# Binary block: the downward product in two halves, and another order of the maxima, clips and output additions

## What is computed

```python
def _quantize_activations_groupwise(x):          # NUM_GROUPS = 5, groups of the batch
    for g in range(NUM_GROUPS):
        ag = x[g * gs:(g + 1) * gs]
        gamma = jnp.max(jnp.abs(ag))
        xq = xq.at[g * gs:(g + 1) * gs].set(jnp.clip(ag * QB / (gamma + EPS), -QB + EPS, QB - EPS))
...
h = _bitlinear(x, W1, b1)          # x @ sign-like W1 + b1, then the quantisation above
h = jax.nn.gelu(h, approximate=False)
out = _bitlinear(h, W2, b2)        # the same again, back to 96 channels
...
t = t + _L2_ffn_ref(_ln_t(t), L2_ffn_W1, L2_ffn_b1, L2_ffn_W2, L2_ffn_b2)
```

## Time and profile before

| | us |
|---|---|
| median of 3 runs | 1110.09 (1109.1 to 1111.11) |
| the profiled execution | 1110.88 |
| its span, first to last instruction | 1109.1 |
| the binary block in it, first upward product to last residual | 689.93 to 771.56 |

### The profile page before, as it was taken

One profiled execution on the slowest core, in us unless ns is written; L12 is line 12 of the kernel. 1 busy time (PEld: TensorE's weight loads), 2 busy tenths in 40 slices (PEclk: granted clock), 3 DMA queues, 4 the chain that ended last, 5 costly groups with the idle time before them and its releaser, 6 DMA issues. The chain is left out here.

```text
span 1109.1 us, 29005 instructions
## 1 busy us (share of the span) xinstructions
PE 1006.5 (91%) x11022; PEld 681.8 (61%) x11022; DVE 676.6 (61%) x1880; ACT 610.5 (55%) x1662; POOL 593.2 (53%) x788
## 2 busy tenths in 40 slices
PE   5999989799979799999999997787988988999998
PEld 2677755467745476767676765455665565566665
DVE  2899944499956355656566663576776686433332
ACT  1666633367733366666666663545665564456553
POOL 4667538477665355454545446344465545373632
PEclk9999999899989999999999998889999999999999
DMA  6500000000000000000000000000000000000000
GB/s 126 97 6 2 2 1 3 1 1 3 1 2 2 1 1 1 2 1 2 1 1 1 2 2 1 2 1 2 1 1 2 2 1 2 2 16 9 16 9 16
DMA packets 28248, 9.65 MB, mean 9 GB/s; under 512 B 26513, under 2 KB 28112, under 8 KB 28112
## 3 DMA queue, kind: packets, MB, share of 16 engines
q1 hardware_dynamic: 25088, 6.89, 3.0%
q10 hardware_dynamic: 3024, 0.92, 0.4%
HBM read 6.23 MB, written 1.57 MB: 7 GB/s over the span
## 5 line engine op out<-in xcount | busy, mean ns | idle before, releaser
L1140 POOL TENSOR_TENSOR fa_e<-fa_e,fa_rc 128x1024 f32<-128x1024 f32 x64 | 120.5, 1893 | 142.3 <-DVE fa_rc L1363 142.3
L1653 POOL TENSOR_TENSOR ca_e<-ca_e,ca_rc 128x256 f32<-128x256 f32 x96 | 76.7, 826 | 84.0 <-DVE ca_rc L1978 84.0
L1297 ACT ACTIVATE fa_e<-bank,fa_nm 128x256 f32<-128x256 f32 x256 | 118.6, 497 | 0.0
L1884 ACT ACTIVATE ca_e<-bank,ca_nm 128x128 f32<-128x128 f32 x192 | 78.0, 430 | 51.0 <-DVE ca_nm L1964 51.0
L2183 ACT ACTIVATE ex_G<-bank,e_b 128x512 f32<-128x512 f32 x96 | 64.4, 687 | 50.2 <-PE bank L137 47.5
L137 PE MATMUL bank<-hT,e_w 96*64 96x512 f32 x384 | 88.6, 596 | 0.0
L2255 DVE SCALAR_TENSOR_TENSOR X<-bank,ex_L,X 128x96 f32<-128x96 f32 x128 | 31.7, 310 | 88.9 <-PE bank L137 82.4
L1357 DVE TENSOR_REDUCE fa_nm<-bank 128x4 f32<-128x1024 f32 x64 | 75.5, 1219 | 14.6 <-PE bank L1166 14.6
L137 PEld LDWEIGHTS bank<-e_w,ex_G 128*64 128x64 f32 x1536 | 67.2, 137 | 17.2 <-issue 10.5
L167 POOL TENSOR_TENSOR ln_r<-ln_v,minus_half 128x2 f32<-128x2 f32 (+2 forms) x85 | 75.7, 890 | 0.0
L186 DVE TENSOR_TENSOR X<-X,bank 128x192 f32<-128x192 f32 (+1 forms) x72 | 30.0, 418 | 71.8 <-PE bank L137 54.2
(11 more groups left out here) (247 smaller groups left out, 2395.1 us busy)
## 6 DMA issues: line engine op xcount, KB each, us to landing
out_tokens<-X SPq DMA_DIRECT2D x8, 192.0 KB, 2.1
X<-in_x SPq DMA_DIRECT2D x14, 96.0 KB, 3.2
e_w<-in_L_ffn_w SPq DMA_DIRECT2D x2, 576.0 KB
bias0r<-in_L_conv_rpb_table ACTq DMA_DIRECT2D x16, 24.0 KB
m0w<-in_L_conv_mlp_w SPq DMA_DIRECT2D x2, 144.0 KB
m1w<-in_L_conv_w SPq DMA_DIRECT2D x2, 144.0 KB
f_w<-in_L_ffn_W SPq DMA_DIRECT2D x2, 142.5 KB
mixer<-in_mixer SPq DMA_DIRECT2D x1, 256.0 KB
```

The costliest lines, as they stand in the source:

```text
L1140: pool.tensor_tensor(e, e, r.broadcast_to([P, 4, TOK]), ALU.mult).then_inc(s["nrm"], 1)
L1297: last = act.activation(E[v % 4][:, i, c, :], bank[b + i][:, c * TOK:(c + 1) * TOK], ACT.Exp, bias=NM[v % 4][:, i, c:c + 1], accum_out=SU[ ...
L1653: last = pool.tensor_tensor(e, e, RC[u % 2][:, images, c, :].broadcast_to([P, 2, (c + 1) * P]), ALU.mult)
L1884: last = act.activation(E[u % 2][:, j, keys(c)], bank[j][:, keys(c)], ACT.Exp, bias=NM[u % 2][:, j, c:c + 1], accum_out=SU[u % 2][:, j, c: ...
```

## The change

- The maximum of the hidden values is taken for each chunk, as soon as the two biases of the chunk are there, into three columns of `parts`; a last reduction makes `am` from them. A semaphore `part` is added.
- The downward product is split: `down(g, b)` does three tiles into bank 6 + b and increments `down` for each half, and the waits on `down` count two a group.
- TensorE's order in iteration g is now: units 4 and 5 of up of g; transposes of g + 1; first half of down of g - 1; spread of the hidden maximum of g; second half of down of g - 1; units 0 to 3 of up of g + 1; `keep_warm` into bank 0; spread of the output maximum of g - 1. The wait for all biases is gone, as is the hidden spread's wait for the output additions. In the first iteration `keep_warm` stands ahead of the spread, into bank 6.
- VectorE's order is now: maximum of g; clips of g; output additions and maximum of g - 1; the rest of the output of g - 1.

```diff
-        def down(g):
+        def down(g, b):
             pe.wait_ge(s["gelu"], KH * (g + 1))
             after(pe, s["z"], 2 * g)
             after(pe, s["ar2"], g)
-            for t in range(GT):
+            for t in range(3):
...
+        up(0, 0, 4)
         for g in range(GROUPS + 1):
             if g < GROUPS:
-                up(g)
+                up(g, 4, 2)
             if g + 1 < GROUPS:
                 tokens(g + 1)
             if g >= 1:
-                down(g - 1)
+                down(g - 1, 0)
             if g < GROUPS:
-                pe.wait_ge(s["h"], 6 * (g + 1))
-                keep_warm(pe, k, bank[2][:], 4)
+                if g == 0:
+                    keep_warm(pe, k, bank[6][:], 4)
                 pe.wait_ge(s["am"], g + 1)
-                after(pe, s["z"], 2 * g)
                 spread(0, 6).then_inc(s["bc1"], 1)
+            if g >= 1:
+                down(g - 1, 1)
+            if g + 1 < GROUPS:
+                up(g + 1, 0, 4)
+                keep_warm(pe, k, bank[0][:], 4)
             if g == GROUPS:
                 next(run)
             if g >= 1:
                 pe.wait_ge(s["am2"], g)
                 spread(1, 7).then_inc(s["bc2"], 1)
...
         def hidden_max(g):
-            dve.wait_ge(s["h"], 6 * (g + 1))
+            for j in range(KH):
+                dve.wait_ge(s["h"], 6 * g + 2 * j + 2)
+                dve.tensor_reduce(parts[:, j:j + 1], H[g % 2][:, j, :], AX.X, ALU.max, apply_absolute_value=True).then_inc(s["part"], 1)
+            dve.wait_ge(s["part"], KH * (g + 1))
             after(dve, s["bc1"], g)
-            dve.tensor_reduce(am[:, 0:1], H[g % 2][:], AX.XY, ALU.max, apply_absolute_value=True).then_inc(s["am"], 1)
+            dve.tensor_reduce(am[:, 0:1], parts[:], AX.X, ALU.max).then_inc(s["am"], 1)
...
         def output(g):
-            dve.wait_ge(s["down"], g + 1)
             after(dve, s["x"], g)
             for b in range(2):
+                dve.wait_ge(s["down"], 2 * g + b + 1)
...
             if g < GROUPS:
                 hidden_max(g)
+                hidden_clip(g)
             if g >= 1:
                 output(g - 1)
-            if g < GROUPS:
-                hidden_clip(g)
-            else:
+            if g == GROUPS:
                 next(run)
             if g >= 1:
                 quantised_output(g - 1)
```

More of the change, by code:

```diff
@@ L216 @@
 LN_SEMS = "var centred rstd y xb x bn ag mv "
-BF_SEMS = LN_SEMS + "tw twe T hT up h am bc1 ar1 c1 clip gelu down z am2 bc2 ar2 c2 zc top0 inv0 top1 inv1"
+BF_SEMS = LN_SEMS + "tw twe T hT up h part am bc1 ar1 c1 clip gelu down z am2 bc2 ar2 c2 zc top0 inv0 top1 inv1"
 CA_SEMS = LN_SEMS + "init T hT ab abe abd vt v sc nm exp rec nrm et ete av ote pj oc bt"
@@ L1430, in binary_ffn @@
     am, ar, cc = sb("am", [P, 2]), sb("ar", [P, 2]), sb("cc", [P, 2, 4])
+    parts = sb("parts", [P, KH])
     half = GT * P // 2
@@ L1455, in tensor, with up @@
     def tensor(pe):
-        def up(g):
+        def up(g, first, count):
             pe.wait_ge(s["hT"], g + 1)
[L1459 to L1463, removed]
-        def down(g):
+            for u in range(first, first + count):
+                j, i = divmod(u, 2)
+                after(pe, s["h"], 6 * g + u - 3)
+                halves(pe, bank[2 + u % 4][:, 0:half], w1T[:, j * P:(j + 1) * P], hT[:, i * half:(i + 1) * half], start=True, stop=True).then_inc(s["up"], 1)
+        def down(g, b):
             pe.wait_ge(s["gelu"], KH * (g + 1))
@@ L1468, in down @@
             after(pe, s["ar2"], g)
-            for t in range(GT):
+            for t in range(3):
                 for j in range(KH):
-                    last = halves(pe, bank[6 + t // 3][:, (t % 3) * C:(t % 3 + 1) * C], H[g % 2][:, j, t * P:(t + 1) * P], w2T[:, j, :],
+                    last = halves(pe, bank[6 + b][:, t * C:(t + 1) * C], H[g % 2][:, j, (3 * b + t) * P:(3 * b + t + 1) * P], w2T[:, j, :],
                                   start=(j == 0), stop=(j == KH - 1))
@@ L1527, in scalar @@
         for g in range(GROUPS):
-            after(act, s["down"], g - 1)
+            after(act, s["down"], 2 * (g - 1))
             for j in range(KH):
```

## The result

The changed kernel takes 1117.15 us (median of 9 runs, 1113.12 to 1118.33) where the kernel before, on the same chips, takes 1111.13: a ratio of 1.0059, 95% interval 1.0047 to 1.0072. It is slower by 6.0 us; 1111.2 and a range of 1107 to 1115 had been forecast. The profiled execution took 1118.01 us with a span of 1116.2.

The account below looks back on a forecast made before the run. No engine was full: a ring of waits bound the kernel, with VectorE losing 2.15 us behind the downward product. Terms -3.70, +4.11, -0.40, +1.10 gave +1.11 us on the median of 1110.09: 1111.2, range 1107.0 to 1115.0.

Parts of the forecast that it names:

- the sum: Whole block: -3.70 up to the last hidden-maximum spread, then +4.11, -0.40 and +1.10, giving +1.11 us.
- The first period: From first to second hidden-maximum spread: VectorE's maximum ready earlier, TensorE free at 9.05; 9.1 against 13.22 us, -4.12.
- the low stretch set aside: Between first and second hidden-maximum spreads: low clock on transposes and half product would make the gain up to 1.4 us less.
- the term for the clock: At the block's end: half clock on the attention's eight transposes behind two idle times, +1.1 us, bounds 0 and 1.65.
- First spread: Start of the block: with the maximum in three parts, the first hidden-maximum spread comes at 698.99 instead of 700.39, -1.40 us.
- Second to fourth period: Later hidden-spread periods: TensorE's queue and low clock hold the output spread; 13.12, 14.49, 14.49 us: -0.15, +1.17, +0.80.
- Extra 0.27 for the parts: VectorE's maximum in each later period: three more instructions cost 0.27 to 0.35 us of the 12.36 us row.
- The end: After the last hidden-maximum spread: attention transposes wait for the output maximum, +4.11; first-half additions overlap, -0.40; clock, +1.1 us.
- low clock twice: Rival, late periods: two low stretches in succession move the output spread from 7.03 to 8.7; +3.3, 1114.5 us; chance 0.25.
- Full clock: Rival, late periods and end: denser filling keeps TensorE fast; periods 13.12 and 13.86, 1108.1 us; chance 0.2.
- the end is covered: Rival, block's end: the following stage doesn't wait for the attention's start, so the 4.11 don't show; 1107.1 us; chance 0.1.

Follow-up runs that it names:

- the run without the four products: The changed kernel without the four filler products (`keep_warm` into bank 0) ahead of the output maximum's spread; 1114.66 us, 1.0035 to the kernel before.
- the run with filler: The changed kernel with twelve more filler products behind the downward product's first half from the third group on; 1114.80 us, 1.0037 to the kernel before.
- The run with the end undone: The changed kernel, with the attention's transposes and first three projections ahead of the output-maximum wait in the last iteration; 1113.47 us, 1.0023 to the kernel before.
- three edits: The changed kernel with attention work ahead of the last wait, no filler ahead of the output spread, filler in TensorE's idle times; 1108.65 us, 0.999 to the kernel before.

## Why the prediction was wrong

In the block the sum gave +1.11 us and +5.27 was measured. Two steps make up the difference. The first period was priced at full clock, with the low stretch set aside without a reason and GpSimd not looked at: 2.18 us. At the end the term for the clock, +1.10, measured 3.56. The other terms came within 0.4 us each, most of them shorter.

- **First spread**: right, 1.32 us against 1.40. Only the last part, 0.95 us, and the last step, 0.16, stood ahead of SP0; the first two parts were taken while TensorE still made the later units.
- **First period, 9.1 forecast, 11.28 measured**: the first step that failed. Its two terms, about 1.5 and 0.7 us, show in the timeline of the changed kernel and in the clock of the stretch:

```profile
704.42 1.51 PE L137 MATMUL bank<-bf_hT,bf_w1T 96*64 96x384 f32 x8 [1.91 <-ACT bf_H L1538]
705.86 1.34 PE L1479 MATMUL bank<-ident,Y 128*96 128x128 f32 x6
707.13 2.83 PE L137 MATMUL bank<-bf_w2T,bf_H 128*64 128x96 f32 x36
709.80 0.39 PE L137 MATMUL bank<-ident,bf_am 128*64 128x128 f32 x4
```

```profile
706.10:709.50 3.40, 3.40 (x36) 3.02 (x36) 1.67 (x3) 1.39 (x4) 2.15 (x3) 0.50 0.02 5
```

  The transposes and the half product ran at half clock (the bound of 1.4 that had been set aside, behind an idle time of 1.91 us), 1.34 and 2.83 for 0.86 and 1.60. The kernel before had it in this period too: its transposes at 707.55 took 1.52 us. The other term had not been seen: with SP0 1.4 us earlier the clips meet GpSimd's multiplication, the first biases and with them the last two units come 5.90 us behind SP0 and not 5.21. Two runs show both: with ten filler products in that wait, and the clock at 1.00, the period fell from 11.28 to 9.67, and with GpSimd's work moved to 9.06. A step moved earlier meets other work than where it stood; the row 697.79 had been read without asking what GpSimd does 3 us later.
- **Second to fourth period**: right in mechanism and size (13.12, 14.49, 14.49 against 12.75, 14.45, 14.33): a ring of VectorE with two answers in it, SP1 held by TensorE's queue, one low stretch behind each of two idle times of 3.2 us. That SP1 of the third came at 7.07 for 7.03 is in part luck: the queue at full clock took 5.35 us and not 5.66, and the low stretch cost more than 1.37 (5.40 in place of 7.07 with filler, 1.67). That each of these idle times brought one is luck too, as the run without the four products shows. The runs with filler and without the four products moved the terms that had been named, by 1.67 and 0.58. In the fourth, the clips of 3.32 us lay beside SP1's wait as worked out. Extra 0.27 for the parts: 2.64 us for the three and 0.16 for the last, the run with the maximum whole has 0.26 less in the second period.
- **The end, +4.81 forecast, +7.26 measured**: the mechanism was right, the transposes wait for an output maximum that had been ahead of the clips; 4.64 us of it against 4.11. The term for the clock, 1.1, was the mis-sized one. It had been priced as one low stretch, on the transposes; the clock was low without a break from 751 to 764, behind the idle times of 4.16 and 1.50 us. It cost 0.53 ahead of the transposes (5.70 us behind SP0; 5.17 forecast, 5.18 in the run with filler), 0.86 on them and 2.17 on the first projections (4.97 for 2.80): 3.56 in all. The run with the end undone, without the second idle time, and the one with filler, with the first cut to 1.47 us, had shorter low stretches there.
- **The rival "low clock twice"** named the right cause at the wrong place: not two stretches ahead of SP1 (SP1 went at 7.07 and 6.95, not at 8.7), but more than one at the end. "Full clock" and "the end is covered" are out.
- **From the block to the whole**: the block is 5.27 us longer, the median 6.0. Behind the block the profiled execution took 339.92 us for 337.54, with more stretches at half clock in the attention. Over all the kernels profiled, whose code there is the same, this stretch goes with its mean granted clock: 337.5 to 337.6 us at 0.98, 338.1 to 338.9 at 0.97, 339.7 to 341.4 at 0.96, 341.9 at 0.95. Why one kernel has more of the low stretches there than another stays open, and with it the 0.7 us.

What the reading missed altogether is larger than what it got wrong: the earlier trace rows were read as a cost that the change would move, not as one that the kernel before paid. The 1.2 GHz on transposes and downward product made up 1.6 of its 13.27 us, and the wait that the change took aim at was 2.15 us of VectorE in a ring that this product ended. Taking the low stretch away in the old order gave 7 us; the new order gave 2.4 with three edits, not clear of no change, and 4.3 with GpSimd's work moved as well.

## What to carry to other kernels

Where a product runs at half clock once a period, look for the idle time in front of it before reordering anything: six filler products in that wait were worth more than the whole new order. Filler too must be priced, as it stands in the queue: four products ahead of a spread cost 0.58 us, sixteen held the next one back. A wait that is put in the middle of an in-order queue must be priced for everything behind it, in the last iteration too, where the next stage's work stands in the same queue. And a step that is moved must be laid beside what the other engines do at its new time, GpSimd included.

## What the runs showed of the hardware

- In the kernel before, TensorE's idle times ahead of the last two units, once a period (1.55 us in the earlier trace rows), were each followed by a stretch at 1.2 GHz. With the parts alone three of four were; the fourth, of 1.55 us, was not. With six filler products in the wait (0 to 1.39 us left) the clock stayed at 1.00 through the four periods of each of three kernels. What the filler does to the clock is shown; which idle time brings a low stretch is not told by its length alone, and stays open.
- Answers of TensorE get slower too: from the end of the maximum to the reduction of its spread VectorE waited 0.54 us at full clock (723.03 in the changed kernel) and 0.80 at half (737.75, 752.07).
- GpSimd's multiplication beside VectorE's clips of SBUF stretched three of them from 1.86 to 2.69 us, and a longer run of GpSimd work to 3.78; reductions of the same tile stayed between 0.919 and 0.954 us each in all periods of the changed kernel, and three took 2.64 us beside GpSimd's work (734.12) as without it (719.66).
